# Paired head groups, whole-tile butterflies, and the second butterfly on GpSimd, in a transformer block on one core

## What is computed

```python
x = x + layernorm(attention(layernorm(x)))        # 16 heads of 32, causal, scores minus the distance
x = x + layernorm(ffn(layernorm(x)))
# ffn: xh = x @ H (Hadamard, 512); xq = xh rounded to 4-bit levels of its row's largest value
#      out = xq @ ternary(weight).T
```

## Time and profile before

| what | value |
|---|---|
| median of 3 runs | 1216.87 us (1216.46 to 1218.15) |
| the profiled execution's own time | 1216.83 us |
| its span on the core | 1215.3 us |
| busy: PE, DVE, ACT, POOL | 91%, 83%, 58%, 49% |
| mean granted TensorE clock | 0.974 |
| one step in the middle of the run | 34.8 us |

### The profile page before, as it was taken

The page is one execution under the profiler, slowest core; times in us unless marked ns, Lnnn a source line. Parts: engine busy times, 40 slices in busy tenths (PEclk is TensorE's granted clock), DMA queues, the critical chain, the costliest instruction groups (busy, mean ns, idle before and its releaser), DMA issues.

```text
span 1215.3 us, 44904 instructions
## 1 busy us (share of the span) xinstructions
PE 1105.3 (91%) x18656; PEld 728.3 (60%) x18656; DVE 1009.3 (83%) x2558; ACT 702.9 (58%) x1494; POOL 595.7 (49%) x715
## 2 busy tenths in 40 slices
PE   5899999999999999999999999999999999999641
PEld 3566556666666666666566666666666666666320
DVE  5748998888988888899888888988888899887772
ACT  5454556665566566655666666556666655665431
POOL 2233545555454556555545555454556555545422
PEclk9999999999999999999999999999999999999875
DMA  9657565665666576656665655666576657654230
GB/s 270 150 119 143 113 138 137 155 133 132 144 124 137 138 149 145 131 132 145 124 139 137 159 135 135 137 127 134 148 139 151 135 127 151 123 115 104 67 70 37
DMA packets 204817, 161.83 MB, mean 133 GB/s; under 512 B 150432, under 2 KB 150688, under 8 KB 204512
## 3 DMA queue, kind: packets, MB, share of 16 engines
q1 hardware_dynamic: 199920, 141.86, 55.1%
q0 software_dynamic: 4688, 17.04, 3.9%
HBM read 40.87 MB, written 16.78 MB: 47 GB/s over the span
## 4 chain that ended last, share of the span: by engine, by line
PE 57%; DVE 31%; issue 7%; ACT 2%; SPq 1%; DMA 1%; POOL 1%; POOLq 0%; DVEq 0%; ACTq 0%
PE f_job L1264 42%; DVE f_bst L963 6%; PE f_st L1363 3%; DVE f_z L1041 3%; PE f_o L1380 2%; PE f_o L1385 2%; PE f_job L1407 2%; DVE f_o L953 2%; DVE f_inverse L955 2%; DVE f_x L987 2%; DVE f_rmax L931 2%; DVE f_folded_x L1004 2%; DVE f_y L995 2%; DVE f_y L994 2%; DVE f_small L989 1%
## 5 line engine op out<-in xcount | busy, mean ns | idle before, releaser
L458 POOL TENSOR_SCALAR_AFFINE_SELECT f_PT<-f_PT 64x512 f32<-64x512 f32 (+1 forms) x256 | 201.0, 809 | 69.6 <-ACT f_PT L618 44.2
L473 POOL TENSOR_TENSOR f_square<-f_stage 128x512 bf16<-128x512 f16 x128 | 130.9, 1044 | 135.4 <-ACT f_stage L596 119.6
L596 ACT ACTIVATE f_stage<-f_job,f_bias 128x256 f16<-128x256 f32 x256 | 106.1, 465 | 88.6 <-PE f_job L1264 81.7
L1264 PE MATMUL f_job<-f_xTh,f_wqh 128*128 128x256 f16 x512 | 140.8, 275 | 15.1 <-DVE f_wkl L794 14.3
L464 POOL TENSOR_TENSOR f_OTl<-f_o,f_OTh 128x256 f16<-128x256 f32 x128 | 86.1, 673 | 115.1 <-ACT f_OTh L636 114.5
L1264 PE MATMUL f_job<-f_xTl,f_wqh 128*128 128x256 f16 x512 | 140.1, 274 | 0.0
L1264 PE MATMUL f_job<-f_xTh,f_wql 128*128 128x256 f16 x512 | 140.1, 274 | 0.0
L1264 PE MATMUL f_job<-f_xTh,f_wkh 128*128 128x256 f16 x512 | 140.0, 273 | 0.0
L1264 PE MATMUL f_job<-f_xTh,f_wkl 128*128 128x256 f16 x512 | 139.9, 273 | 0.0
L1264 PE MATMUL f_job<-f_xTl,f_wkh 128*128 128x256 f16 x512 | 139.8, 273 | 0.0
L917 DVE SCALAR_TENSOR_TENSOR f_stage<-f_job,f_bias,f_stage 128x256 f16<-128x256 f32 x256 | 110.7, 474 | 31.7 <-ACT f_stage L596 29.7
(11 more groups left out here) (180 smaller groups left out, 3033.3 us busy)
## 6 DMA issues: line engine op xcount, KB each, us to landing
f_stacks<-f_stage SPq DMA_DIRECT2D x384, 128.0 KB
f_xin<-x SPq DMA_DIRECT2D x32, 512.0 KB, 4.7
f_x<-x SPq DMA_DIRECT2D x32, 512.0 KB, 3.9
out<-f_z POOLq DMA_DIRECT2D x32, 512.0 KB, 3.4
f_Vmix<-f_V SPq DMA_DIRECT2D x32, 256.0 KB
f_Vmix<-f_V SPq DMA_DIRECT2D x64, 128.0 KB
f_stacks<-rows_const SPq DMA_DIRECT2D x3, 512.0 KB, 9.3
f_stacks<-wqT SPq DMA_DIRECT2D x2, 512.0 KB, 5.8
```

What stands on the lines that cost most here:

```text
L458: nc.gpsimd.affine_select(out=d, in_=d, compare_op=ALU.is_ge, fill=0.0, base=odd * SUB, pattern=[[0, 4], [0, TP], [1, SUB]], channel_multi ...
L473: nc.gpsimd.tensor_tensor(square[:, 2 * m + pair, :], h, h, ALU.mult).then_inc(squared, 1)
L596: nc.scalar.activation(stage[:, 2 * m, g, :], bank("qk", g)[:, m * W2:(m + 1) * W2], ACT.Identity, bias=bias[:, m, g:g + 1]).then_inc(qk_h ...
L1264: mm = pe.matmul(dst, lhs[a](c), rhs[b](c), start=(n == 0), stop=(n == 3 * KC - 1))
```

## The change

Two head groups are taken at a time by `invert`, `normalise`, `heads_high` and `heads_low` (a width w of 2, or 1 in the last step), on PSUM banks that are now one tensor. `fold`, `x2_high`, `x2_low` and `turn_x2` take both token tiles in one instruction each instead of one per tile. `fold_again` moves from VectorE to GpSimd, between clear_future(s, 2) and clear_future(s, 3), ahead of `z_root`. VectorE's order is changed, and on TensorE weigh(s, 2) goes from the end of step s to the next step, ahead of weigh(s, 3).

```diff
-        ps_o = [ps("o0"), ps("o1")]
+        ps_pair = ctx.enter_context(nc.psum_tensor("f_o", [P, 2, D], F32))
+        ps_o = [ps_pair[:, i, :] for i in range(2)]
...
-            def turn_x2(k, t):
-                sp.wait_ge(x2l_made, TP * k + t + 1)
-                until(sp, h_product, TP * (k - 1) + t + 1)
+            def turn_x2(k):
+                until(sp, h_product, TP * k)
                 for half, src in enumerate((x2h, x2l)):
-                    sp.dma_start(x2T[half][:, t], src[:, t, :], transpose=True).then_inc(x2_turned[t], 16)
+                    sp.wait_ge((x2h_made, x2l_made)[half], k + 1)
+                    sp.dma_start(x2T[half][:].rearrange("p t c n -> p (t c) n"),
+                                 src[:].rearrange("p t n -> p (t n)"), transpose=True).then_inc(x2_turned, 16)
...
+            def fold_again(k):                                   # GpSimd
+                pool.wait_ge(halved, 2 * k + 2)
+                until(pool, x2l_made, k)
+                quarters = y[:].rearrange("p t (h q n) -> p (t h) q n", h=2, q=2)
+                turned = folded_x[:].rearrange("p t (h q n) -> p (t h) q n", h=2, q=2)
+                left, right = quarters[:, :, 0], quarters[:, :, 1]
+                nc.gpsimd.tensor_tensor(turned[:, :, 0], left, right, ALU.add).then_inc(folded, 1)
+                nc.gpsimd.tensor_tensor(turned[:, :, 1], left, right, ALU.subtract).then_inc(folded, 1)
...
                 clear_future(s, 2)                               # GpSimd, the loop
+                if has(k):
+                    fold_again(k)
+                clear_future(s, 3)
                 if has(k - 1):
                     z_root(k - 1)
-                if has(s):
-                    clear_future(s, 3)
-                    heads_low(s, 0)
-                    heads_low(s, 1)
+                heads_low(s, 0, 2)
                 if has(k - 1):
                     finish_out(k - 1)
-                if has(s):
-                    heads_low(s, 2)
...
                 exps(s, 2, 0)                                    # ScalarE, the loop
-                invert(s, 1)
+                invert(s, 0, 2)
                 if has(k - 1):
                     keep_q(k - 1, 1)
                 exps(s, 2, 1)
                 keep_v(n, 0)
-                if has(k):
-                    x2_high(k, 0)
-                    x2_high(k, 1)
-                heads_high(s, 0)
                 exps(s, 3, 0)
                 exps(s, 3, 1)
+                if has(k):
+                    x2_high(k)
                 keep_v(n, 1)
+                heads_high(s, 0, 2)
                 if has(k - 1):
                     norm_z(k - 1)
-                invert(s, 2)
-                heads_high(s, 1)
-                heads_high(s, 2)
...
                 qk_low_part(n, 0)                                # VectorE, the loop
                 if has(k):
-                    normalise(k, 3)
+                    normalise(k, 2, 2)
                 qk_low_part(n, 1)
...
                     y_out(k, 1)
                     y_stats(k)
-                normalise(s, 0)
                 if has(k):
                     residual(k)
                 if has(k - 1):
                     scale_out(k - 1, 0)
                 if has(k):
-                    fold(k, 0)
-                    fold_again(k, 0)
-                    fold(k, 1)
-                    fold_again(k, 1)
+                    fold(k)
                 if has(k - 1):
                     scale_out(k - 1, 1)
                     z_stats(k - 1)
-                if has(k):
-                    x2_low(k, 0)
-                normalise(s, 1)
                 maxima(n, 0)
                 maxima(n, 1)
                 keep_norms(n)
+                if has(k):
+                    x2_low(k)
+                normalise(s, 0, 2)
                 if has(k - 1):
                     z_columns(k - 1)
-                if has(k):
-                    x2_low(k, 1)
                 maxima(n, 2)
                 maxima(n, 3)
                 split_max(n)
-                normalise(s, 2)
                 if has(k):
                     x_stats(k)
...
                     qk(n, 0)                                     # TensorE, the loop
+                    weigh(k, 2)
                     weigh(k, 3)
...
                 values(n, 1)
-                weigh(s, 2)
                 scores(n, 2)
                 scores(n, 3)
```

More of the change, by code:

```diff
@@ L92, in score_bank @@
         def score_bank(n, i):
-            return bank("s", i) if n else (ps_st + ps_o)[i]
+            return bank("s", i) if n else (ps_st[i] if i < 2 else ps_o[i - 2])
         W = {n: (sb(f"w{n}h", [P, KC, D], F16), sb(f"w{n}l", [P, KC, D], F16)) for n in "qkvo"}
@@ L231, in fast_path @@
         folded = sem("folded")
-        x2_turned = [sem(f"x2_turned{t}") for t in range(TP)]
+        x2_turned = sem("x2_turned")
         x2h_made = sem("x2h_made")
@@ L519, in _ @@
             clear_future(last, 2)
-            heads_low(last, 0)
+            fold_again(last - 1)
+            z_root(last - 2)
             clear_future(last, 3)
[L522 to L525, removed]
+            heads_low(last, 0, 2)
+            heads_low(last, 2, 1)
+            heads_low(last, 3, 1)
             finish_out(last - 2)
             y_root(last)
+            fold_again(last)
             z_root(last - 1)
@@ L623, in exps, with invert, heads_high, x2_high @@
                                          scale=1.0 / SS).then_inc(expd, 1)
[L625 to L642, removed]
+            def invert(s, g, w):
+                slots = slice(g % 2, g % 2 + w)
+                act.wait_ge(pv_done, 4 * s + g + w)
+                until(act, o32_made, 4 * s + g + w - 2)
+                nc.scalar.activation(inverse[:, slots, :], ps_pair[:, slots, W2:D], ACT.Ln).then_inc(log_made, w)
+                act.wait_ge(log_made, 4 * s + g + w)
+                nc.scalar.activation(inverse[:, slots, :], inverse[:, slots, :], ACT.Exp,
+                                     scale=-1.0).then_inc(inverse_made, w)
+            def heads_high(s, g, w):
+                act.wait_ge(o32_made, 4 * s + g + w)
+                nc.scalar.activation(OT[s % 2][0][:, g:g + w, :], o32[:, g % 2:g % 2 + w, :],
+                                     ACT.Copy).then_inc(OTh_made, w)
+            def x2_high(k):
+                act.wait_ge(folded, 2 * k + 2)
+                until(act, q_turned, TP * k)
+                nc.scalar.activation(x2h[:], folded_x[:], ACT.Copy, scale=SX).then_inc(x2h_made, 1)
             def round_levels(k, t):
@@ L689, in _ @@
                 if has(k):
-                    invert(k, 3)
+                    invert(k, 2, 2)
                 qk_high_part(n, 1)
@@ L752, in _ @@
             level(last - 2, 1)
-            invert(last, 0)
             exps(last, 2, 0)
+            invert(last, 0, 2)
             keep_q(last - 2, 1)
@@ L757, in _ @@
             exps(last, 3, 0)
-            invert(last, 1)
-            heads_high(last, 0)
-            x2_high(last - 1, 0)
             exps(last, 3, 1)
-            x2_high(last - 1, 1)
-            invert(last, 2)
-            heads_high(last, 1)
+            heads_high(last, 0, 2)
+            x2_high(last - 1)
+            invert(last, 2, 1)
             norm_z(last - 2)
-            invert(last, 3)
-            heads_high(last, 2)
-            heads_high(last, 3)
+            invert(last, 3, 1)
+            heads_high(last, 2, 1)
+            heads_high(last, 3, 1)
             round_levels(last - 1, 0)
@@ L774, in _ @@
             keep_q(last - 1, 1)
-            x2_high(last, 0)
-            x2_high(last, 1)
+            x2_high(last)
             norm_z(last - 1)
@@ L945, in split_max, with normalise @@
                   .then_inc(max_parts, 1)
[L947 to L959, removed]
+            def normalise(s, g, w):
+                slots = slice(g % 2, g % 2 + w)
+                dve.wait_ge(inverse_made, 4 * s + g + w)
+                until(dve, OTl_made, 4 * s + g + w - 2)
+                heads, sums, inv = ps_pair[:, slots, 0:W2], ps_pair[:, slots, W2:D], inverse[:, slots, :]
+                nc.vector.tensor_tensor(heads, heads, inv, ALU.mult).then_inc(o_scaled, w)
+                dve.wait_ge(o_scaled, 4 * s + g + w)
+                nc.vector.tensor_tensor(inv, sums, inv, ALU.mult).then_inc(o_error, w)
+                dve.wait_ge(o_error, 4 * s + g + w)
+                nc.vector.scalar_tensor_tensor(o32[:, slots, :], inv, 2.0, heads,
+                                               ALU.subtract, ALU.mult).then_inc(o32_made, w)
             def statistics(which, src, mv):
@@ L989, in residual, with fold @@
                 note(nc.vector.scalar_tensor_tensor(y_off[k % 2], y_mv[:, :, 0], -1.0, y_rstd, ALU.mult, ALU.mult))
[L991 to L1004, removed]
+            def fold(k):
+                dve.wait_ge(x1_made, TP * k + TP)
+                left, right = x1[k % 2][:, :, 0:W2], x1[k % 2][:, :, W2:D]
```

(24 more changed lines are left out.)

49 lines of the change are left out of this document (21 added, 28 removed).

## The result

The changed kernel takes 1255.4 us (median of 4 runs, 1252.7 to 1256.8) against 1217.4 before on the same chip (4 runs, 1216.5 to 1218.2): a ratio of 1.031, 95% interval 1.029 to 1.032. It is slower by 38 us. The forecast was 1242, slower at 0.59, range up to 1256: the sign and the mechanism of the holds come true, and the size is 13 us short.

The account below looks back on a forecast made before the run. The prediction took the loop through VectorE's path from y_out(k, 1) to qk_low_part(n, 1) as the bound. From 1216.8 us, +21 for the loop and +4 at the end gave 1242 us, full range 1188 to 1256.

Parts of the forecast that it names:

- point 1: VectorE's normalise taken in pairs, two 512-wide triples instead of four groups: -0.8 us on the path.
- point 5: Without normalise(s, 0) covering GpSimd's y_root, VectorE's residual waits for it: +0.84 us; L989 stays held as before, 0.
- points 2, 3: VectorE's path loses fold_again, -1.36 us, and has fold over both tiles in two 512-wide instructions, -0.34.
- point 6: fold_again's two additions on GpSimd hold z_stats' small VectorE instructions L1046 and L1048: +1.9 us, from below 0 to 2.5.
- point 7: Paired heads_low and the last addition on GpSimd hold VectorE's split_max (L940, L943): +1.65 us, between 0.3 and 3.
- point 4: x2_low made whole on VectorE, one instruction of 1.32 us against two at about 0.6: 0.
- The rest: Stretch from TensorE's qk(n, 3) to the next y_out(k, 1), without a stall: 10.07 us, kept in the period.
- 28 x 0.75: TensorE waits 0.75 us for qk(n, 3) in each of the loop's 28 steps: +21 us.
- The end: Last block and last step, where VectorE waits for GpSimd's additions and ScalarE's x2_high: +4 us, between 0 and 6.
- A: Rival: GpSimd's reads hold nothing that matters, TensorE becomes the bound: 1190 us, between 1178 and 1202; chance 0.28.
- B: Rival: only one hold bites, L943 slips in or norm_z is late: 1217 us, within 3; chance 0.15.
- C: Rival: both additions hold at split_max, or weigh(s, 1) waits too; from 1.3 us a step, 1259 us; chance 0.05.

Follow-up runs that it names:

- experiment 1: Changed kernel with z_stats' two small instructions moved to right after find_scale, where GpSimd is idle: 1206.5 us, ratio to the kernel before 0.990.
- experiment 4: Changed kernel with fold_again back on VectorE, over both tiles, right behind fold: 1244.5 us, ratio to the kernel before 1.021.
- the other three experiments: Changed kernel with finish_out moved behind the next front_root, 1266.3 us; that plus early z_eps, 1244.1; or fold_again back on VectorE, 1244.5.

## Why the prediction was right, and where its size was off

By stretches of the path in one step, before from 549.36 and after from 563.20, the triples of normalise taken out and counted by themselves:

| stretch | forecast | measured |
|---|---|---|
| triples (point 1) | -0.8 | -0.46 |
| y_out to fold (point 5, L989) | +0.84 | +0.46 |
| fold to scale_out(k-1, 1) (points 2, 3) | -1.70 | -0.98 |
| scale_out to z's statistics (point 6) | +1.9 | +1.46 |
| L936 to x's statistics (point 7) | +1.65 | +1.27 |
| all others (point 4) | 0 | -0.08 |
| sum | +1.9 | +1.67 |

**Point 1.** Dependent 512-wide instructions stand 0.79 apart (577.26, 578.05), not 0.73, and the second triple has a gap of 0.47 that the trace puts down to its own first instruction and doesn't explain. **Points 2 and 3.** The additions left VectorE as forecast, but the select that had held L989 now meets the fold: L991 is held for 0.46, and scale_out then waits 0.20 for TensorE. **Point 5.** The root is uncovered for 0.82, forecast 0.84; net it is +0.46 as L985 (L989 before) is no longer held, which I had at 0. The hold wasn't removed, it moved down to L991. **Point 4** held: 1.21 for two at about 0.6. **Points 6 and 7.** The mechanism is right: four instructions held, each for what was left of GpSimd's instruction. The sizes are smaller: L1033 comes 0.73 after L480 starts, not 0.6, so is held 0.42, and L1035 for 1.04; L936 for 0.43, L939 for 1.01. "The Trainium skill", page "SBUF — State Buffer", section "Who interferes with whom", says that the later instruction blocks for the whole of the other; the edges in the two timelines agree in the ordinary step (the 1.91 us of first steps, below, go past one instruction), and taking one pair of holds away was worth 49 us (experiment 1).

This step's path is one of the longer ones, 25.24; the mean of ordinary steps is 24.9 where the prediction said 25.4. **The rest** was taken as constant: 10.07 from qk(n, 3)'s first matmul on, 10.2 from the path's end; it is 10.70 from the path's end. That is the step of the prediction that failed: ScalarE's queue hangs on VectorE's path (front_offset 591.29, front_norm 591.47, then rounding, two stages, x2's level at 594.27), and TensorE's turn_q now waits for that level (19.6 us, before 5.2). From qk(n, 3)'s first matmul (588.50) to `y_out(k, 1)` are 10.64: of the 0.57 more, 0.25 are ahead of turn_q (it starts 6.60 after that matmul, before 6.35), and 0.32 behind it, where `keys` waits for ScalarE's next exponentials (twice, 0.19 and 0.20). I had put ScalarE at 0. That its queue is the cause is read from the timelines; no run moved it. The two errors cancel by luck, and the ordinary step is 35.62, forecast 35.6. The wait of weigh(s, 2), which I called hidden, is there too (17.5 us over 26 steps); in experiment 4 it is 18.1 us over 28 steps.

**Where the missing 13 us are.** 28 x 0.75 was one price for all steps. Ordinary steps did cost 0.79, but the seven first steps 1.73: in them VectorE waits 1.10 for TensorE before scale_out(k-1, 1), where the ordinary step waits 0.20, and the holds on z_stats' two instructions take 2.2 instead of 1.5. The select comes later there and pushes the additions later against z_stats. L481 starts at 643.57, with z_stats' first instruction, and the next select at 644.80; that instruction is held past both the addition and the select's first half, and the other one by its second.

```profile
643.57 1.91 DVE L1033 SCALAR_TENSOR_TENSOR f_small<-f_x_mv,f_small 128x2 f32<-128x2 f32 x1
```

First steps cost 7 us more than forecast. The end took 6.6 instead of 4. The first `y_out(k, 1)` comes 2.8 us later, 2.6 of them left where the loop starts, which wasn't forecast: the granted clock there is lower, in the windows (columns as above) first of the kernel after, then of experiment 1:

```profile
36.00:56.00 20.00, 17.28 (x270) 12.61 (x267) 14.99 (x34) 6.39 (x15) 4.77 (x5) 0.91 0.41 102
```

```profile
36.00:56.00 20.00, 16.64 (x277) 12.65 (x275) 16.21 (x37) 7.43 (x17) 4.77 (x5) 1.00 0.53 137
```

It is at its lower level, 0.50 (1.2 GHz), from 42 to 45 us, after TensorE had stood idle for 2.3 us until 40.57 for restacked tiles. It is there again from 59 until near 69 us, where experiment 1 is back at 1.00 (2.4 GHz) near 64. Whether the change itself causes that is open; experiment 1, with nearly the same start of the program, reaches its first `y_out(k, 1)` as early as before (93.83 and 93.86 us, against 96.64), and the other three experiments are between (94.86 to 95.90).

**The rivals.** A, where small instructions slip between GpSimd's, is refuted for this kernel by the means of 602 to 1203 ns, and experiment 1, with two of the four holds gone, came to 1206, toward its 1190. B needed L939 at 0.19; it took 1.20. C's price fits the first steps only, 1.7 us each, and there by another way: its extra is at z_stats, while L939 is held as in the other steps. (The chances of "slower" add up to 0.61 by the prediction's own parts, 0.52 + 0.05 + 0.04, not 0.59.)

## What to carry to other kernels

When elementwise work moves to GpSimd, list VectorE's instructions that will stand beside it, the tiniest first: one of 0.15 us took up to 1.91 here once it was held, and what queues behind it pays. Such small ones that depend on early data can be moved to where GpSimd is idle; two instructions moved were worth more here than the whole change had cost. And before a store or a load is moved, follow it further: which load must wait for it, which small instruction then stands beside it, and what other transfers then run at the same time.

## What the runs showed of the hardware that was not expected

- A 128x2 VectorE instruction of 0.15 us took 1.91 us in every first step: L1033 at 643.57 was held through an addition and the first half of the select behind it, and was not let through at the edge between them. In the ordinary step it was let through at the edge between L480 and L481 (571.64), and only the next one was held by L481. What decides between the two isn't shown.
- A hold can move instead of going: 0.46 us went from L989 to L991 in the change, and in 9 of 25 steps of experiment 1 from L991 to GpSimd's select (2.42 against 1.83). Experiment 1's own two instructions show that it can also go: 0.16 us each.
- The same 128x2 instructions were held by a select (L1038 and L1040 of experiment 4, means of 465 and 440 ns) as by an addition.
- A 128x512 float32 addition took 1.27 us on GpSimd and 0.68 on VectorE (L480 of the kernel after, L996 of experiment 4). "The Trainium skill", page "GPSIMD Engine Reference", section "Engine selection", gives about twice as slow; the rows agree. That ratio was not what it cost: the holds were.
